# One image's feed-forward and the next image's attention on one core: the order of the products around the projections, the attention tiles and the router's exponential

## What is computed

```python
x = x + conv_ref(ln_c(x), ...)         # normalised over channels
    # qkv = 1x1 conv; agg = 5x5 depthwise then grouped 1x1; ms = [qkv, agg]
    # 64 heads of 8: q, k = relu; kv = k^T [v, 1]; out = q kv; out / its last column
    # 1x1 projection, batch norm
t = tokens(x)
t = t + ffn_ref(ln_t(t), ...)
    # token_repr = x.mean(axis=1); probs = softmax(token_repr @ router_w.T); top 2 -> weights of 6 experts
    # h = gelu(x @ W1 + b1); out = sum over experts of weight * (h @ W2 + b2)
```

## Time and profile before

| | |
|---|---|
| median of three runs | 1650.11 us (1649.84 to 1651.37) |
| the profiled execution | 1651.42 us, of which the span of the instructions is 1649.7 us |
| PE matmuls busy | 1360.8 us, 82% |
| DVE busy | 1278.6 us, 78% |
| ACT busy | 1063.1 us, 64% |
| POOL busy | 972.8 us, 59% |
| mean granted TensorE clock | 0.93 of full |

### The profile page before, as it was taken

The page is one execution under the profiler, slowest core; times in us unless marked ns, Lnnn a source line. Parts: engine busy times, 40 slices in busy tenths (PEclk is TensorE's granted clock), DMA queues, the critical chain, the costliest instruction groups (busy, mean ns, idle before and its releaser), DMA issues.

```text
span 1649.7 us, 18712 instructions
## 1 busy us (share of the span) xinstructions
PE 1360.8 (82%) x6844; PEld 786.7 (48%) x6844; DVE 1278.6 (78%) x1305; ACT 1063.1 (64%) x1855; POOL 972.8 (59%) x746
## 2 busy tenths in 40 slices
PE   4516647799888988799888988899888997999598
PEld 2315525455455545455455545555464445545343
DVE  4895999997969966996969966996969987970000
ACT  3434534677567775767567776777567866675476
POOL 3683626576487566576477566676476647444544
PEclk8756879899999999999999999899999999999899
DMA  5100000000001000010001100010001000100000
GB/s 180 77 2 25 26 0 1 1 27 13 1 1 39 31 9 1 0 64 14 1 1 39 39 1 1 1 39 13 1 1 39 13 1 1 39 13 1 0 14 26
DMA packets 14251, 32.75 MB, mean 20 GB/s; under 512 B 2384, under 2 KB 5328, under 8 KB 13904
## 3 DMA queue, kind: packets, MB, share of 16 engines
q1 hardware_dynamic: 14160, 31.56, 5.5%
HBM read 23.17 MB, written 8.39 MB: 19 GB/s over the span
## 4 chain that ended last, share of the span: by engine, by line
PE 46%; DVE 19%; ACT 19%; POOL 9%; issue 6%; DMA 1%; SPq 0%; POOLq 0%; ACTq 0%; DVEq 0%
PE wbk L533 19%; DVE dacc L1112 15%; PE acc L546 11%; PE wbk L625 6%; ACT gh L730 4%; ACT hb L731 4%; POOL dwo L930 3%; PE wbk L635 3%; ACT tapb L705 2%; POOL nrm L889 1%; PE wbk L584 1%; ACT hb L825 1%; PE wbk L611 1%; ACT dwo L700 1%; PE wbk L599 1%
## 5 line engine op out<-in xcount | busy, mean ns | idle before, releaser
L1112 DVE SCALAR_TENSOR_TENSOR dacc<-qkvs,dww,dacc 128x930 f32<-128x930 f32 (+4 forms) x954 | 1053.2, 1186 | 0.0
L960 POOL TENSOR_TENSOR gl<-hb,gh 128x512 f16<-128x512 f32 x256 | 304.4, 1191 | 419.1 <-ACT hb L731 418.2
L825 ACT ACTIVATE hb<-wbk,b1s 128x512 f32<-128x512 f32 x256 | 175.2, 684 | 156.3 <-PE wbk L533 156.2
L930 POOL TENSOR_TENSOR dwo<-dwo,tapb 128x992 f32<-128x992 f32 (+1 forms) x104 | 240.4, 2311 | 12.9 <-ACT tapb L705 9.7
L546 PE MATMUL acc<-gh,w2h 128*128 128x512 f16 x512 | 197.6, 386 | 33.5 <-ACT sum_b L764 30.6
L546 PE MATMUL acc<-gh,w2l 128*128 128x512 f16 x512 | 197.9, 387 | 0.0
L546 PE MATMUL acc<-gl,w2h 128*128 128x512 f16 x512 | 197.9, 386 | 0.0
L730 ACT ACTIVATE gh<-hb,ewg 128x512 f16<-128x512 f32 x256 | 182.3, 712 | 9.5 <-DVE ewg L1065 9.5
L533 PE MATMUL wbk<-th,w1h 128*128 128x512 f16 x512 | 154.2, 383 | 33.7 <-ACT qr L807 16.7
L731 ACT ACTIVATE hb<-hb,ewg 128x512 f32<-128x512 f32 x256 | 181.8, 710 | 0.0
L1016 DVE RECIPROCAL den<-den 128x128 f32<-128x128 f32 x32 | 30.4, 949 | 189.1 <-ACT den L804 189.1
(11 more groups left out here) (146 smaller groups left out, 2232.1 us busy)
## 6 DMA issues: line engine op xcount, KB each, us to landing
xa<-x SPq DMA_DIRECT2D x8, 1024.0 KB, 5.0
yr<-x SPq DMA_DIRECT2D x8, 1024.0 KB, 5.0
out<-yr SPq DMA_DIRECT2D x16, 512.0 KB, 2.8
dwo<-w SPq DMA_DIRECT2D x1, 2048.0 KB, 11.0
yr<-w SPq DMA_DIRECT2D x2, 1024.0 KB, 16.3
dwo<-w_qkv SPq DMA_DIRECT2D x1, 768.0 KB, 4.7
wp<-w_proj SPq DMA_DIRECT2D x1, 512.0 KB, 12.4
pw<-w_pw SPq DMA_DIRECT2D x16, 24.0 KB
```

Source lines behind the costliest of these rows:

```text
L825: last = nc.scalar.activation(hb[:, f % GB, :], b[:], ACT.Gelu, bias=b1s[:, f % FT:f % FT + 1], scale=1.0 / (X_SCALE * W_SCALE))
L930: ins = nc.gpsimd.tensor_tensor(d3[:, oy, ox], d3[:, oy, ox], t3[:, iy, ix], ALU.add)
L960: nc.gpsimd.tensor_tensor(gl[:, f % GB, :], hb[:, f % GB, :], gh[:, f % GB, :], ALU.subtract).then_inc(g_low, 1)
L1112: ins = nc.vector.scalar_tensor_tensor(out=dst[:, oy, ox], in0=i3[:, jy, jx], scalar=dww[:, m, tap:tap + 1], in1=a3[:, oy, ox], op0=ALU.mu ...
```

## The change

Only `schedule()` is changed; the same 1736 items are given, in another order.

- In the second half of an attention (`att new 1 t`) the four items `qkv j 0` and `qkv j 1` stand between the tiles, behind tiles 1, 4, 5 and 7, where they stood behind all eight. One feed-forward block moves from behind tile 5 to behind them. Image j's first `base` items are given one block earlier.
- The projections stand between the blocks: back (half 0), proj 0 0, block, proj 0 1, block, back (half 1), proj 1 0, block, proj 1 1.
- In the first half of an attention (`att j 0 t`) the items `qkv nxt 2` and `qkv nxt 3` stand between the tiles. `scale j 0 0` now stands ahead of `rbc` and `apply`.
- Behind `low` and ahead of `back j 0` a feed-forward block is given, the first of image `new`.
- Ahead of `exp new` all second products of image new-1 are given, with its `final`. The next second product then comes with the fifth block of image `new`, as before.

```diff
-                if i >= LAG:
-                    second(i - LAG)
+                if i - finished[0] >= LAG:
+                    second()
...
             for t in range(TT):
                 give(("att", new, 1, t))
-                if t in (2, 5):
+                if t == 2 or (t == 5 and not d):
                     fill(1)
+                if t in (1, 4, 5, 7):
+                    give(*qs[:1])
+                    del qs[:1]
...
         if c:
             fill(1)
             give(("back", new, 1, 0, 0), ("back", new, 1, 0, 1))
+            give(("proj", new, 0, 0), *out[0], *toks[:2])
+            fill(1)
+            give(("proj", new, 0, 1), *toks[2:4])
             fill(1)
             give(("back", new, 1, 1, 0), ("back", new, 1, 1, 1))
+            give(("proj", new, 1, 0), *out[1], *toks[4:6])
             fill(1)
-            give(("proj", new, 0, 0), *out[0], *toks[:2])
-            give(("proj", new, 0, 1), *toks[2:4])
-            give(("proj", new, 1, 0), *out[1], *toks[4:6])
             give(("proj", new, 1, 1), *toks[6:])
...
-        if d:
-            give(*[("att", j, 0, t) for t in range(4)], n=n)
-        if c:
-            fill(1 if d else 2)
+        ks = qkv(nxt, 2) + qkv(nxt, 3) if c and a else []
+        for t in range(TT if d else 0):
+            give(("att", j, 0, t), n=n)
+            if t in (1, 2, 5, 7):
+                give(*ks[:1])
+                del ks[:1]
+            if t == 3:
+                give(("scale", j, 0, 0))
+                if c:
+                    give(("rbc", new, 1, 0), ("rbc", new, 1, 1), ("apply", new, 1, 0), ("apply", new, 1, 1))
...
             give(("low", new, 1, 0), ("low", new, 1, 1))
-            if a:
-                give(*qkv(nxt, 2))
+            fill(1)
         if d:
             give(*[("back", j, 0, ch, g) for ch in range(NCH) for g in range(2)], n=n)
         if c:
             give(("logits", new))
-            if a:
-                give(*qkv(nxt, 3))
-            else:
-                fill(1)
             fill(left(new - 1) + 2)
+            while finished[0] < new * (NCH * FT):
+                second()
             give(("exp", new))
```

More of the change, by code:

```diff
@@ L88, in schedule @@
     unsplit = []
+    finished = [0]
     def give(*items, n=1):
@@ L266, in schedule @@
     give(("gsplit",) + stream[-1])
-    for i in range(k - LAG, k):
-        second(i)
+    while finished[0] < k:
+        second()
     return o
```

20 lines of the change are left out of this document (11 added, 9 removed).

## The result

The changed kernel takes 1724.68 us (median of four runs, 1723.69 to 1729.07) against 1650.74 us for the kernel before in the same comparison: ratio 1.0449, 95% interval 1.0425 to 1.0473. It is 74 us slower. The forecast was 1696 us, with a range up to 1716: the direction was right, the size was 46 instead of 74 us, and the time lies outside the range. The profiled execution has a span of 1722.0 us, 72.3 more than before.

The account below looks back on a forecast made before the run. PE was taken as nearest to bounding, the late-emptied acc costing 7.3 us a stage. Terms 9.0 + 21.6 + 4.0 + 2.8 + 2.7 + 6.0 = 46.1 us gave 1696 us from the median; range 1668 to 1716, slower 0.88.

Parts of the forecast that it names:

- Stages 0 and 1: Stage 1: most new PE waits fall on time DVE takes anyway; only later logits hold up the routing, 2.7 us.
- Projections and tiles: Stages 2 to 7: projections wait 0.5 us more, twice, bank waits between tiles lose 0.6; 1.5 a stage (bounds 0, 2.5).
- Tile 0 to block 5, stages 2 to 5: First attention tile to block 5: 13.65 + 19.5 against 5.2 + 22.6 us, 5.4 lost per stage, 21.6 in all.
- the same, stages 6 and 7: Same walk without the sums, in stage 7 also without qkv items: 4.0 and 2.8 us lost, an estimate.
- Block 5 to the next stage: Rest of a stage behind block 5: no term in the sum, so 0.
- Tail: Stage 8, one chain: squares 3.6 us later, logits behind block 0 and a second product; 6.0 us taken.
- second rival: Same waits but cheap: clock stays up (16 us less), projections' waits nil (9 less), 1671 us; chance 17%.
- Agg items to block 5: ACT 9.3, scaled copies 1.3, differences 2.4, sums 4.7, last half of statistics 1.8: 19.5 us, against 22.6 before.
- ACT's chain: Behind the last second product: emptying acc, table load, exponentials, emptying agg items, squares, second table load, Gelu: 9.3 us.
- the walk: Item-by-item timing of the new order; in stage 8 it put image 7's first second product 6.5 us later.
- third (faster): Block 0's input comes as PE gets there, the 7.8 and 2.3 us vanish: about 1634 us; chance 8%.
- The fourth: Slower still: clock stays at 1.2 GHz through transposes and logits into block 1 and a second product: 1714 us; 9%.

Follow-up runs that it names:

- the flush alone: Kernel before, with the earlier image's remaining second products and the emptying of acc given ahead of exp, all else as before: 1664.22 us, ratio 1.0061.
- the projections alone: Kernel before, with only the changed kernel's order of back items, blocks and projections, without the block ahead of the last projection: 1671.65 us, ratio 1.0128.
- the two runs with idle work: Overwritten matmuls added ahead of waits: to the changed kernel at block 0 and projections, 1714.41 us; to the kernel with both moves at back items, 1636.93 us.
- with rnorm earlier: Kernel with both moves plus overwritten matmuls at the back items, changed to give rnorm with its statistics, not one block later: 1654.75 us, ratio 1.0023.
- with both moves: Kernel before, with second squares and sums first, second products and acc's emptying behind them after the agg items, statistics one block earlier: 1641.54 us, ratio 0.9948.

## Why the prediction was right and wrong

Right were the sign and the mechanism, item by item.
- Block 0 of image 3 starts 20.66 us after the first attention tile (predicted 20.7), behind a wait for POOL's `low` of 7.59 us (7.8), and it runs at a clock of 0.50.
- The agg items start at 33.4 (34.35). ACT empties acc directly ahead of the table load, and the third bank waits 1.95 us ("about 2").
- The two projections wait 1.90 to 1.93 us, half a microsecond more each.
- DVE's busy time stayed (1278.6 and 1282.2 us) and its wait for attention tiles grew, from 189.1 to 212.7 us.

Wrong were the sizes. The 72.3 us of span against the sum of 46.1:

| Term | predicted | measured |
|---|---|---|
| Stages 0 and 1 | 2.7 | 3.3 (-3.6 and +6.9) |
| Projections and tiles (first stretch, stages 2 to 7) | 9.0 | 17.6 |
| Tile 0 to block 5, stages 2 to 5 | 21.6 | 28.1 |
| the same, stages 6 and 7 | 6.8 | 8.2 |
| Block 5 to the next stage | 0 | 5.0 |
| Tail | 6.0 | 10.1 |

The first row is right by luck. Stage 1 lost 6.9 us and not 2.7, for it has the projections' waits too, which the sum counts only from stage 2 on. Stage 0 hides it: it ends at 219.7 us and not at 223.3, though the items up to there are the same. Other kernels with the same items reach that place at 222.1 (the flush alone) and 220.1 us (the projections alone), so these 3.6 us are for the most part no effect of the change.

The steps that failed:

1. **The projections' term** had the waits and left out the clock. Where the clock stayed up (stages 4 and 6) the loss is 1.8 us, close to the 1.5 predicted; in stages 2, 3, 5 and 7 the third projection runs at half speed and the loss is 3.5. Undoing this part gave 16.0 us. The prediction's bound of 2.5 us a stage was too narrow, though it had named clock losses behind waits of 2 us in its second rival, as something that might be moved rather than added. They were added.
2. **Agg items to block 5**: 19.5 predicted, 21.9 in stage 4. A second clock loss stands behind the wait for the third agg bank (3.10 us for the second 16 products, 1.95 for the first 16), and the sums took 5.6 us where 4.7 were put in, the second of them beside DVE's tap (last section). The prediction's 9.3 us for ACT's chain also add up to 9.1 only.
3. **After block 5**: the prediction assumed that a stage's rest was untouched. In stage 6 it is 3.6 us longer: PE waits there for ACT's Gelu and for a copy, each of which stands behind a tap (L715) in ACT's queue. PE in that stage, at two waits that the kernel before doesn't have there, and the lower clock behind the second (0.79 for two products, 0.59 at full speed):

```profile
1314.40 1.16 PE L594 MATMUL wbk<-pw,dwo 128*128 128x128 f32 x8 [1.66 <-ACT hb L835]
1317.15 0.79 PE L543 MATMUL wbk<-th,w1h 128*128 128x512 f16 x2 [1.59 <-ACT vt L802]
```

4. **The tail**: `rbc` took 3.48 us at a low clock for the 16 products that take 2.02 at full speed, and the first half of the statistics 3.75 where 916.52 above has 2.02. From the statistics to block 0 that makes 3.8 us, all of it clock. Block 0's wait of 9.65 us is no loss by itself: before, PE waited 6.67 us at the logits and 1.98 at block 0, with 1.00 of logits between. Behind block 0 another 2.4 us are lost up to the first second product, which comes 10.0 us later in all where the walk had 6.5. Only the later squares (3.9 us at the statistics, 3.6 predicted) were sized right. A row of the kernel before:

```profile
1544.78 1.00 PE L649 MATMUL wbk<-rws,us 128*128 128x11 f32 x4 [6.67 <-ACT th L715]
```

Together: PE is busy 18.1 us longer. The sum had put in 2.3 us of new clock loss and taken out 2.6 us of the old in each stage, nearly nothing in net. By this account some 18 of the 26 us that are missing are clock, and the other 8 are waits. As an account of time that is argued and not shown: in the two runs with idle work PE's busy time fell by far more than the time did (28 against 10 to 14 us, 18 against 4.6). Shown are the 10 to 14 us that came back when two kinds of wait were filled.

The rivals: the second (cheap, 1671) and third (faster) fell. The fourth gave 1714, near to the time but not by its mechanism: behind block 0 the clock was back at full by 890.8, ahead of the transposes at 891.44, so that nothing here tells whether transposes would have lifted it. The loss came from more places with a low clock, not from longer ones. The flush alone, 12.8 us slower, shows that the loss is not only the price of block 0's new place: removing the acc wait in this way doesn't pay by itself.

## What to carry to other kernels

Cost a new wait on TensorE as the wait plus a possible stretch at half speed behind it; in this kernel waits of 1.9 us added up to 1.7 us more each, and not in every stage. Count what the clock gives back in the kernel's time and not in busy time (28 us of busy time gave 10 to 14 of time, 18 gave 4.6). When one wait is removed and nothing is gained, look for a second chain that ends at the same place, and shorten both together (no gain from either alone, 0.5% from both, with a third small move). When an item waits, try to give the waiting item later before moving the job that it waits for ahead, since that job's queue has other customers (5 us gained against 18 lost).

## What the runs showed of the hardware

- The clock fell behind single waits of 1.9 us, and behind two of 1.66 and 1.59 us close together (stage 6 above). A projection behind a wait of 1.9 us took either 3.67 or 5.37 us, nothing between: 5.37 in 4 of 12 cases in the changed kernel's stages 2 to 7 and in 6 of 12 with the projections alone. Neither the length of the wait nor the order of the items decides it: in one execution the same 16 products behind the same wait of 1.95 us took 2.05 us in stage 3 and 3.68 in stage 4.
- POOL and DVE disturbed each other at one kind of tap, the unclipped one (128x1024, `dacc<-qkvs,dww,dwo`). It is the one tap with both inputs in SBUF, `qkvs` and `dwo`; all others take `dacc` as their second input, which the kernel keeps in PSUM (`psum_tensor`). DVE's pair of such taps takes 2.49 us while POOL is idle and 6.25 beside the sums, both in the changed kernel:

```profile
838.62 2.49 DVE L1114 SCALAR_TENSOR_TENSOR dacc<-qkvs,dww,dwo 128x1024 f32<-128x1024 f32 x2
...
914.52 6.25 DVE L1114 SCALAR_TENSOR_TENSOR dacc<-qkvs,dww,dwo 128x1024 f32<-128x1024 f32 x2
```

In the traces of all runs such a tap took 1.28 to 1.30 us wherever POOL had no arithmetic under way, and up to 3.40 where it had. An operation of POOL took some 1.0 us longer beside it: the second half of the sums 3.33 instead of 2.35 us, and with rnorm earlier even one on 128x8:

```profile
887.50 1.19 POOL L894 TENSOR_TENSOR sv<-st 128x8 f32<-128x8 f32 x1
```

The same operation with both moves, clear of that tap:

```profile
884.56 0.20 POOL L887 TENSOR_TENSOR sv<-st 128x8 f32<-128x8 f32 x1
```

The Trainium skill, "SBUF — State Buffer", in its section "SBUF: two separate sides", says that VectorE and GpSimd share one pair of ports, which one of them holds for a whole instruction, and that a VectorE operation with two inputs in SBUF needs it too, against a GpSimd operation that reads SBUF. The traces agree: beside the clipped taps, which have one input in SBUF and one in PSUM, no operation of POOL was longer by half a microsecond (POOL's differences kept their 1.16 us), and the taps kept their 1.1 to 1.3 us. The one other place where POOL was slowed is in stage 0, beside DVE's operations `w1l<-dwo,w1h` and `w2l<-yr,w2h`, which have both inputs in SBUF as well: `xl` took 4.16 us in place of 2.13. No run changed where a tap's inputs lie, so the cause is read from which operations are slow and not from an experiment.
